# The low part of a q or k projection: between the two row maxima of a batch, or behind both

## The reference

```python
t = x.reshape(B, C, H * W).transpose(0, 2, 1)
q, k, v = jnp.split(t @ w_qkv + b_qkv, 3, axis=-1)
scores = jnp.einsum('bhnd,bhmd->bhnm', q, k) / jnp.sqrt(jnp.float32(hd))
out = jnp.einsum('bhnm,bhmd->bhnd', jax.nn.softmax(scores, axis=-1), v)
out = out.transpose(0, 2, 1, 3).reshape(B, C, H, W) ...
out = out @ w_o + b_o
```

## Time and profile before

| | us |
|---|---|
| median of three runs | 4700.89 (4694.37 to 4705.71) |
| the profiled execution, device time | 4708.2 |
| its span, first to last instruction | 4706.5 |
| TensorE's matmuls busy | 4131.9 (88%) |
| VectorE busy | 2695.5 (57%) |
| GpSimd busy | 2641.3 (56%) |
| ScalarE busy | 1942.2 (41%) |
| mean granted clock of TensorE | 0.963 |

### The profile page before, as it was taken

One profiled execution on the slowest core, in us unless ns is written; L12 is line 12 of the kernel. 1 busy time (PEld: TensorE's weight loads), 2 busy tenths in 40 slices (PEclk: granted clock), 3 DMA queues, 4 the chain that ended last, 5 costly groups with the idle time before them and its releaser, 6 DMA issues.

```text
span 4706.5 us, 69143 instructions
## 1 busy us (share of the span) xinstructions
PE 4131.9 (88%) x21822; PEld 2468.9 (52%) x21822; DVE 2695.5 (57%) x2771; ACT 1942.2 (41%) x3504; POOL 2641.3 (56%) x1303
## 2 busy tenths in 40 slices
PE   0599989998899989999899998999989998899979
PEld 0355546555465645556455564555546565464645
DVE  4345664557635576456755566455664657636575
ACT  0244443544435444353434434344443544435443
POOL 0166465745657357573565646565565745757357
PEclk9899999999999999999999999999999999999999
DMA  7211213111121211212120121211102121121212
GB/s 261 74 43 50 85 31 103 37 66 63 45 89 37 77 56 50 86 37 81 52 91 35 48 86 37 91 49 68 67 30 100 37 72 61 46 86 46 81 50 74
DMA packets 147413, 314.94 MB, mean 67 GB/s; under 512 B 17600, under 2 KB 30400, under 8 KB 136512
## 3 DMA queue, kind: packets, MB, share of 16 engines
q1 hardware_dynamic: 147008, 309.92, 19.6%
HBM read 259.54 MB, written 50.33 MB: 66 GB/s over the span
## 4 chain that ended last, share of the span: by engine, by line
PE 69%; DVE 14%; issue 10%; ACT 3%; DMA 2%; POOL 1%; DVEq 0%; ACTq 0%; SPq 0%; POOLq 0%
PE aux_ps L1019 28%; PE score_ps L1104 15%; PE acc_ps L1118 15%; PE aux_ps L1060 7%; DVE den L951 4%; DVE mxp L924 3%; DVE o_t L956 2%; PE aux_ps L1128 2%; DMA xin<-in_x_dram 1%; DMA w_split<-o_t 1%; PE aux_ps L1069 1%; DVE xin L885 1%; POOL xs L546 1%; ACT v_y L713 1%; ACT xin L653 1%
## 5 line engine op out<-in xcount | busy, mean ns | idle before, releaser
L563 POOL TENSOR_TENSOR sums<-sums,probs 128x1024 f32<-128x1024 f32 x768 | 1833.6, 2388 | 1000.7 <-ACT probs L691 960.4
L924 DVE TENSOR_REDUCE mxp<-aux_ps 128x2 f32<-128x1024 f32 x1041 | 1273.4, 1223 | 1424.3 <-PE aux_ps L1060 1412.3
L691 ACT ACTIVATE probs<-score_ps 128x512 f32<-128x512 f32 x2048 | 1058.6, 602 | 860.1 <-PE score_ps L1104 859.5
L1118 PE MATMUL acc_ps<-probs,v_y 128*64 128x512 f32 x4096 | 1028.8, 624 | 0.0
L1019 PE MATMUL aux_ps<-xs,w_qk 128*128 128x512 f32 x3168 | 865.9, 412 | 40.8 <-DMA w_qk<-w_split 40.8
L1060 PE MATMUL aux_ps<-k_hi,q_hi 64*128 64x512 f32 x2082 | 498.8, 472 | 393.5 <-DVE mxp L924 132.0
L1019 PEld LDWEIGHTS aux_ps<-xs,w_qk 128*128 128x128 f32 x3168 | 569.2, 191 | 448.3 <-issue 300.9
L563 POOL TENSOR_TENSOR sums<-probs 128x1024 f32<-128x1024 f32 x128 | 304.6, 2380 | 757.6 <-ACT probs L691 757.6
L1060 PEld LDWEIGHTS aux_ps<-k_hi,q_hi 64*128 64x128 f32 x2082 | 207.6, 190 | 670.1 <-DVE mxp L924 278.6
L1118 PEld LDWEIGHTS acc_ps<-probs,v_y 128*64 128x64 f32 x4096 | 254.4, 139 | 480.6 <-issue 418.6
L951 DVE RECIPROCAL den<-den 128x256 f32<-128x256 f32 (+1 forms) x240 | 443.9, 1850 | 7.7 <-ACT den L702 7.7
(11 more groups left out here) (111 smaller groups left out, 2994.3 us busy)
## 6 DMA issues: line engine op xcount, KB each, us to landing
xin<-in_x_dram SPq DMA_DIRECT2D x280, 256.0 KB, 3.0
w_qk<-w_split SPq DMA_DIRECT2D x134, 512.0 KB, 4.2
w_v<-w_split SPq DMA_DIRECT2D x34, 1024.0 KB, 6.8
w_o<-w_split SPq DMA_DIRECT2D x32, 1024.0 KB, 7.0
w_split<-o_t SPq DMA_DIRECT2D x16, 1024.0 KB, 5.5
y<-v_y SPq DMA_DIRECT2D x64, 256.0 KB, 2.0
v_y<-in_x_dram SPq DMA_DIRECT2D x64, 256.0 KB, 2.9
xin<-y SPq DMA_DIRECT2D x64, 256.0 KB, 2.8
```

Source lines behind the costliest of these rows:

```text
L563: pool.tensor_tensor(sums[h][:, :], a, probs[:, g % SLOTS_P, :], ALU.add).then_inc(c_sum[h].sem, 1)
L691: act.activation(probs[:, n % SLOTS_P, token_half(u % 2)], score_ps[:, u % SCORE_BANKS, :], ACT.Exp, scale=SCALE).then_inc(c_exp.sem, 1)
L924: dve.tensor_reduce(mxp[:, :, n, h], ps, AX.X, ALU.max).then_inc(c_free["D"].sem, 1)
L1118: last = nc.tensor.matmul(acc_ps[head(j), :], v_y[:, m, head(2 * p + j)], probs[:, n % SLOTS_P, token_half(j)], start=(m == 0), stop=(m == ...
```

## The change

VectorE executes `lows(b - 1)` in the second turn of the loop over the two maxima, not in the first:

```diff
@@ -982,7 +982,7 @@
                             max_slot(i, t, p, s)
                             if s == 15:
                                 combine(i, t, p)
-                            if j == 0 and b:
+                            if j == 1 and b:
                                 lows(b - 1)
                         for part in range(2):
                             if phase_at(b, RECIP + part) is not None:
```

## The result

The changed kernel takes 4747.93 us (median of 4 runs, 4736.96 to 4749.93) against 4701.07 of the kernel before: a ratio of 1.0097, 95% interval 1.0083 to 1.0111. The forecast was 4739 with a range of 4708 to 4758. The profiled executions took 4749.93 and 4708.2, their spans are 4748.2 and 4706.5. That is 41.7 more, to be found in the traces.

A forecast was written before the change was run, and what follows sets the result against it. TensorE, with 69% of the chain, was taken as the bound. Terms 6.5 + 5.2 + 20.3 + 6.0 + 1 - 0.5 = 38.5 on the median 4700.89 gave 4739, range 4708 to 4758.

The forecast's parts named there:

- Batches 11 and 27: Nothing covers the low part, so TensorE gets bank 2 late in 3 batches an image: 24 x 0.27 = 6.5 lost.
- batches 1 modulo 4: On-time odd batches: a denominator ahead of TensorE's next tile in bank 2 covers the low part; cost nothing.
- Hyperbolic batch 19: VectorE has no idle before batch 20's first maximum, so the low part lengthens its queue: 8 x 0.65 = 5.2 lost.
- Euclidean batch 19: L885 arrives some 0.6 later, waits for GpSimd's sum in every image, and batch 20 lasts 13.05 in each: 20.3 lost.
- The inner value: The 20.3 taken for Euclidean batch 19, between bounds 5 and 26, from the third image's batch 20 of 13.05.
- Hyperbolic batch 22: L956 comes behind GpSimd's sum in the four images where it got in first: 4 x 1.5 = 6.0 lost.
- Euclidean batch 15: L791 will wait for GpSimd's sum instead of L792: 8 x 0.1 = 1 lost.
- Batches 7 modulo 8: The transposition of the row maxima lies ahead of TensorE's tile in bank 2 and covers the low part; cost nothing.
- one sign of being wrong: Busy times changing at all on instructions other than L885, L956, L791 and GpSimd's sums would show the prediction wrong.
- Only the queue's shift: Rival: Euclidean batch 19 costs only 5 and batch 22 nothing, 17 in all, giving 4718; chance 0.25.
- More than that: Rival: idle ahead of batch 20 grows in images with a clock drop, and ties turn elsewhere; 4754 and more; chance 0.12.
- Faster: Rival: sums move so that L956 gets in first in batches 2 modulo 4; 4681 with 40 turns; chance 0.04.

The follow-up runs named there:

- experiment 2: Low part behind both maxima only in batch 19 of the hyperbolic pass, otherwise the kernel before: 4710.89, ratio 1.0024.
- (4): The changed kernel, with the low part of the Euclidean batch 19 still later, between the two scalings L885: 4724.56, ratio 1.0045 to the kernel before.
- (5): The changed kernel, with GpSimd's second sum of the Euclidean batch 19 cut to 8 of 1024 columns: 4726.35, ratio 1.0045 to the kernel before.
- experiment 11: Low part behind both maxima only in batches 1, 5 and 7 modulo 8, otherwise the kernel before: 4711.17, ratio 1.0016.
- Experiments 3: Low part behind both maxima in all odd batches but 19, otherwise the kernel before: 4715.55, ratio 1.0032.
- experiment 1: Low part behind both maxima only in batch 19 of both passes, otherwise the kernel before: 4742.62, ratio 1.0095.
- the first group: Unchanged runs of the kernel before, on the same chip as the first set of follow-up kernels: median 4699.73.

## Why the prediction was right

**The direction and the size.** All terms of the sum held within 1.4 of their size, and one was missing. On the median 38.5 was forecast and 47 measured, in the traces 41.7; TensorE's waits for the row maxima grew by 22.8, where 15 to 25 was forecast.

**Batches 11 and 27.** The forecast of 24 waits of 4 in all is there with 24 and 4.4, and the length grew by 0.25 each (0.27). Where another tile covers the low part, batches 1 modulo 4 and 7 modulo 8, TensorE waits for it nowhere, and VectorE's idle has grown to 0.85 as forecast ("nearly 0.9").

**Hyperbolic batch 19.** Right with 5.05, and experiment 2 has it alone.

**Euclidean batch 19.** Right in size (20.4 for 20.3) and in mechanism, shown from both sides: with the low part moved off L885's way (4), and with the sum taken away (5). The inner value came from one image of eight that was already in the state which the change makes the rule. That the sizes agree to 0.1 is luck: batch 20 alone grew by 24.7, to 13.6 on the mean and not 13.05, and batch 19 gave 4.25 back, which was not forecast. In the kernels in which nothing was moved in either batch, the two together differ from before by 3.8 for each long L885 more or less, and by up to 3.3 besides (experiment 11).

**Hyperbolic batch 22.** Right in its cause, experiment 2, and 4.6 for 6.0: four images became 1.3 longer, not 1.5, and the other four, long already, 0.1 to 0.2 shorter. But "four of eight images are of the short kind" was read off one execution as if it belonged to the program. In the next there were six.

**Euclidean batch 15.** L791 waits in L792's place as forecast, and it costs 0.24 an image, not 0.1:

```profile
2312.51 1.85 DVE L791 TENSOR_TENSOR sc<-sc 128x128 f32<-128x128 f32 x1
2314.40 0.29 DVE L792 TENSOR_TENSOR sc<-sc,ss 128x128 f32<-128x128 f32 x1
```

**The one step that failed** is "Batches 7 modulo 8 ... I cost them at nothing too". That is right for bank 2, but the reciprocal behind the low part of batch 31 comes 0.4 to 0.5 later. In the Euclidean pass GpSimd's multiplication (L570) waits for it, and in GpSimd's queue the last sum, a scaling of the hyperbolic output (L577) and its addition (L580) stand behind. L956 at the pass's end meets that addition. In the fourth image, before and then after:

```profile
2428.39 1.11 DVE L956 SCALAR_TENSOR_TENSOR o_t<-o_raw,bias_q,o_t 128x512 fp32r<-128x512 f32 x1 [5.66 <-ACT o_t L707]
...
2427.66 1.29 POOL L580 TENSOR_TENSOR v_y<-v_y,xin 128x512 f32<-128x512 f32 x1 [0.16 <-POOL xin L577]
...
2451.46 1.59 DVE L956 SCALAR_TENSOR_TENSOR o_t<-o_raw,bias_q,o_t 128x512 fp32r<-128x512 f32 x1 [5.19 <-ACT o_t L707]
...
2451.22 1.29 POOL L580 TENSOR_TENSOR v_y<-v_y,xin 128x512 f32<-128x512 f32 x1 [0.16 <-POOL xin L577]
```

L956 ends 0.55 and 0.54 behind the addition. The first output tile starts 0.47 later, 8 x 0.47 = 3.7. Experiments 3 and 11 have the same with 3.9 and 3.8, and experiment 1, where the low part of batch 31 stayed in its place, does not have it. That the delay goes by way of GpSimd's queue is read from the order of the starts; it wasn't tried by itself.

**Two readings that were off.** The 112 waits for row maxima are not "seven for each of the 16 passes": 12 of them, 20.0 long, lie ahead of the first pass, and a pass has four to seven. No term was built on it. And one sign of being wrong came true by its letter, that busy times change on instructions other than those named. L792 lost 16.3 over the run, as the paragraph on batch 15 says itself, and the matmuls of L1118 went from 624 to 627 ns on the mean. TensorE's matmuls are busy longer where the clock is lower: 9.29 in the fourth image's batch 20 at 0.87, and 7.59 before at 1.00. On VectorE no instruction but L791, L792, L885 and L956 changed by more than 1 over the run.

**The rivals.** "Only the queue's shift" fell with experiment 1. Of "More than that" one half was there in part: the longest waits grew to 5.5 in two batches 20, which were 14.71 and 14.50 long, but batch 19 gave most of that back. I found no turned ties elsewhere. With 47 the measured time lies between it and the forecast. "Faster" needed the sums to move against L956 to its good; at batch 22 that happens and goes away by chance, for 6 at most.

## What to carry to other kernels

Look into what hole an instruction falls before it is moved: the low part cost nothing between the two maxima because VectorE waited there anyway, and behind them up to 0.67 in the batches where VectorE had no idle time to make up for it. Then look at what comes behind it in that queue, and whether one of those instructions only just gets in ahead of another engine: 0.6 of delay became 2.5 an image there. The same reading shows where a hole is still free, and a longer instruction was worth more in it: moving L956 gave 2.5%.

## What I had not expected

Two executions of one program differ in who wins: L885 starts 0.01 to 0.03 behind GpSimd's sum and gets in, so by the recorded starts it is not simply the first one that wins; at 0.12 or more it waits for 2.1 us. One, then three of eight images fell on the bad side. In the traces of the other kernels it gets in at up to 0.08, while an L956 at 0.07 or 0.08 waits. At 3.8 an image two more such images are over 7 us of 4700, as much as the standard deviation of the runs of the kernel before in the first group (7.0, from 4688.66 to 4715.61). A single profile does not say how many ties a program loses.

A wait that grows from 1.7 to 3.8 us costs more than its growth: in the fourth image batch 20 became 3.8 longer for 2.1 of it, the rest being matmuls at the lower clock (0.87 granted on the mean of the batch against 1.00). But the wait is not the whole of it: before the change the first image's batch 20 had a clock of 0.78 with a wait of 1.8. What lowered it there I did not follow.
